# Both scans' output rows turned by VectorE, ahead of the next carry instead of behind it or through TensorE

## The chip, the cores and the metric

The kernel runs on one core of one Trainium2 chip. The time is the device time of one execution in microseconds; the time before is the median of 3 runs. The profile is of one further execution. Engines are named as in the profile: PE (TensorE matmul; PEld its weight loads), DVE (VectorE), ACT (ScalarE), POOL (GpSimd) and SP (SyncE, which here only issues DMAs). A q behind a name (SPq, ACTq) is that engine's issuing side.

## The reference

The input x is 16 images of 64 rows, 128 columns and 64 channels in float32. Two residual blocks follow each other:

```
x = x + mix(groupnorm(x)) + bias     # mix: along the 128 columns, one softmax matrix for each of 4 heads
x = x + scan(groupnorm(x))           # scan over the 64 rows of an image, one after the other

carry = row[0]                       # an output row too
carry = row[h] + relu(conv1d_9(carry))      # h = 1..63: 9 taps along the 128 columns, 64 x 64 channels
```

Both group norms are over the whole image in 32 groups of 2 channels, so a scan can begin only when its images are mixed. Each scan row needs the one before it.

## The kernel before, in words

The images go in two waves of 8. First the 8 images of wave 0 are loaded, normalised and mixed with no scan beside them (until about 183 us). Then wave 0 is scanned, 64 rows for 8 images at once, while the 8 images of wave 1 are loaded, normalised and mixed beside it: one image for each iteration of 8 rows ("the first scan" below). Last, wave 1 is scanned with nothing beside it ("the second scan", from about 548 us). Each engine's program is written out by hand in its own order; engines meet only at semaphores (wait_ge, then_inc). An engine's instructions run in that order, so one that waits holds up all behind it.

Data of a scan row lie with two neighbouring columns times 64 channels on the 128 partitions. A row is split in two halves, s = 0 and s = 1, of 4 images each (NS = 2, SW = 256 elements a partition). For each half of each row:

- PE convolves (convolve, L1037 and L1041): 15 products of 256 columns, five each of wh with carry_h, wl with carry_h, and wh with carry_l. carry_h is the carry written as fp32r, carry_l the rest.
- DVE makes the new carry in L825: the larger of the convolution and 0, plus the normalised row. It waits for conv_done, every fourth row for rows_ready, and for total_ready, which says that the carry before has been read.
- ACT rounds the carry into carry_h (L543); DVE subtracts the two into carry_l (L835).
- POOL adds the carry to the unnormalised row: total (add_carry, L410), the output row. It may overwrite total only when the row before has been turned.
- ACT normalises one image's next group of four rows into rows (norm_rows, L513).

total has columns and channels on the partitions and must be turned before it is stored. Before the change this is done in two ways. In the first scan PE turns row t-1 by four 128 x 128 transposes into ps_out, behind the convolution of half 0 of row t (turn_out, L1029); ACT copies ps_out to staged (stage_out, L523), and SP stores it with two DMAs of 128 KB in pieces of 512 bytes (store_row, L303). In the second scan DVE turns each half in blocks of 32 x 32 (flip_out, L812), right behind the carry of the next row's same half, and the row is stored by eight DMAs of 32 KB in pieces of 128 bytes, five issued by SP (L314) and three by ACT (L533). staged has two buffers, taken in turn, so a turn of row h waits until the stores of row h-2 have landed.

In the first scan DVE has the preparation of the next image between these (prep, with a gap number for its place in the row: gap 0 and 2 behind the carry of half 0 and 1, gap 1 and 3 behind carry_l): statistics (L638, L739), the mixed sum of a quarter image (L732, behind half 1 of odd rows) and small operations for the group norms. PE has the mix (L949) and the turning of the mixed rows (L962) behind half 1, POOL the scaling for the mix (L379), and ACT the copying of the mixed rows (L491).

The order in DVE's program before, around the carry:

```
dve.wait_ge(conv_done[s], t + 1)
...
nc.vector.scalar_tensor_tensor(carry[s][:, :], ...).then_inc(carry_ready[s], 1)
if wave == 1 and not (is_zero(it) and i == 0):
    flip_out(wave, it, i, s)
if b is not None:
    prep(b, e, it, i, 2 * s, prev, more)
if not (last and i == STEPS - 1):
    dve.wait_ge(high_ready[s], t + 2)
    nc.vector.tensor_tensor(carry_l[s]...).then_inc(low_ready[s], 1)
```

Of the kernel before, what the change touches and what calls it, by code (L numbers as in the profile page):

```python
# [15 lines left out]
def mix_and_scan_kernel(nc: bass.Bass, x: bass.AP, centers: bass.AP, spreads: bass.AP,  # L16
# [8 lines left out]
    B, H, N, C = x.shape  # L25
# [33 lines left out]
    out_pairs = out.rearrange("b h (j q) c -> b h j (q c)", q=2)  # L59

    with ExitStack() as ctx:
# [139 lines left out]
        out_turned = sem("out_turned")  # L201
        out_staged = sem("out_staged")
        stored = [sem(f"stored{n}") for n in range(2)]
# [60 lines left out]
        def _(sp):  # L264
# [30 lines left out]
            def store_row(wave, h, t, buf):  # L295

                staged_rows = held(sp, t)
                alone(sp, w_zeroed)
                sp.wait_ge(out_staged, staged_rows)
                src = staged[:, buf, :].rearrange("p (m f) -> p m f", f=P)  # L300
                for e in range(2):
                    dst = out_pairs[wave * W + e:(wave + 1) * W:2, bass.ds(h, 1), :, :]
                    sp.dma_start(dst.rearrange("m h j f -> (h j) m f"),  # L303
                                 src[e * J:(e + 1) * J, :, :]).then_inc(stored[buf], 16)

            def store_flipped(wave, h, buf):

                rows_flipped = held(sp, h + 1)
# [3 lines left out]
                for block in range(SP_BLOCKS):  # L312
                    dst, src = flipped_block(wave, h, buf, block)
                    sp.dma_start(dst, src).then_inc(flip_stored[buf], 16)  # L314

            def iteration(wave, it, b, e, more):


                for i in range(STEPS):
                    if wave == 1 and not (is_zero(it) and i == 0):  # L320
                        store_flipped(wave, it * STEPS + i - 1, (i + 1) % 2)
                    if wave == 0 and not (is_zero(it) and i == 0):
                        store_row(wave, it * STEPS + i - 1, (it + wave * ITERS) * STEPS + i, (i + 1) % 2)
                    if i == 1 and more >= 1:
                        load_chunk(b + 1, 1 - e, CH - 1, CH * b)
                    if i in (3, 5, 7) and more >= 2:
                        load_chunk(b + 2, e, (i - 3) // 2, CH * b + (i - 3) // 2 + 1)

# [7 lines left out]
            store_row(0, H - 1, H, 1)  # L336
# [4 lines left out]
            for n in range(2):  # L341
                sp.wait_ge(stored[n], H // 2 * 32)
                sp.wait_ge(flip_stored[n], H // 2 * 128)
# [3 lines left out]
        def _(pool):  # L347
# [53 lines left out]
            def add_carry(wave, it, i, s):  # L401
                t = (it + wave * ITERS) * STEPS + i
                pool.wait_ge(carry_ready[s], t + 1)
                if wave == 0 and not is_zero(t):
                    pool.wait_ge(out_turned, t)
                if wave == 1 and is_zero(it) and i == 0:
                    pool.wait_ge(out_turned, t)
# [717 lines left out]
```

## Time and profile before

| | |
|---|---|
| median of 3 runs | 787.57 us (785.27 to 787.59) |
| the profiled execution | 787.0 us |
| its span, first to last instruction | 785.2 us |
| mean granted clock of TensorE | 0.978 of full |
| PE, DVE, ACT, POOL busy | 703.5, 580.8, 524.2, 421.0 us |
| transferred | 68.11 MB, 87 GB/s over the span |

The page's list of costliest groups gives for each line and engine the operation, the tiles it writes and reads, the number, the busy time, the mean of one, the idle time ahead of it and what ended that. Lists in order of time give start, length, engine, line, operation and tiles, with the idle time ahead of the first and what ended it in square brackets. The length of an operation runs from its start to its end; an engine may start the next a little before the end of the last, so the distance of two starts is what an operation costs the engine.

### The profile page before, as it was taken

How to read it: one execution, taken by the hardware profiler on the slowest of the kernel's cores; microseconds unless marked ns; L12 is line 12 of the kernel's file. 1: busy time of each engine (PE TensorE's matmuls, PEld its weight loads, DVE VectorE, ACT ScalarE, POOL GpSimd, SP SyncE). 2: the span in 40 equal slices, each digit the busy share in tenths (PEclk: the TensorE clock that was granted, in tenths of full speed). 3: DMA queues.
4: the chain of work that ended last, by engine and by line, in shares of the span. 5: the costliest groups of instructions: out<-in, count | busy, mean ns of one | idle time of the engine just before them, and what ended most of it. 6: DMA issues, size and time to landing. Idle time of an engine off the chain costs nothing.

```text
span 785.2 us, 18039 instructions
## 1 busy us (share of the span) xinstructions
PE 703.5 (90%) x5356; PEld 671.4 (86%) x5356; DVE 580.8 (74%) x1298; ACT 524.2 (67%) x918; POOL 421.0 (54%) x416
## 2 busy tenths in 40 slices
PE   1577777767999999999999999995999999999996
PEld 1466666667999999999999999995999999999996
DVE  7589999955868787786868777664766767777775
ACT  1167767785877777777777777756566666666661
POOL 1555566623655556565656565661455555555553
PEclk9889999998999999999999999998999999999999
DMA  9846556132434443444434431221344444444444
GB/s 179 157 109 133 122 121 134 28 81 49 100 76 101 108 95 84 94 108 94 93 81 107 96 80 43 53 56 27 52 74 76 71 73 74 71 75 68 78 69 80
DMA packets 307594, 68.11 MB, mean 87 GB/s; under 512 B 274772, under 2 KB 307540, under 8 KB 307540
## 3 DMA queue, kind: packets, MB, share of 16 engines
q1 hardware_dynamic: 255316, 61.15, 38.0%
q10 hardware_dynamic: 52224, 6.30, 5.2%
q8 instruction: 26, 0.43, 0.2%
q14 instruction: 28, 0.23, 0.1%
HBM read 33.85 MB, written 33.55 MB: 86 GB/s over the span
## 4 chain that ended last, share of the span: by engine, by line
PE 58%; DVE 15%; issue 11%; ACT 7%; ACTq 6%; POOL 1%; SPq 0%; DVEq 0%; DMA 0%; POOLq 0%
PE ps_conv L1037 26%; PE ps_conv L1041 13%; PE ps_mix L949 9%; PE ps_in L962 6%; ACTq L533 5%; DVE st L638 5%; PE ps_out L1029 3%; ACT x_paired L491 2%; DVE carry L825 2%; ACT carry_h L543 2%; PE ps_small L939 2%; DVE x_sb L732 2%; DVE st L739 2%; ACT rows L513 1%; DVE rows L732 1%
## 5 line engine op out<-in xcount | busy, mean ns | idle before, releaser
L410 POOL TENSOR_TENSOR total<-x_paired,carry 128x256 f32<-128x256 f32 x256 | 234.2, 915 | 256.6 <-DVE carry L825 145.8
L835 DVE TENSOR_TENSOR carry_l<-carry,carry_h 128x256 fp32r<-128x256 f32 x252 | 166.1, 659 | 82.6 <-ACT carry_h L543 74.1
L543 ACT ACTIVATE carry_h<-carry 128x256 fp32r<-128x256 f32 x252 | 105.5, 419 | 162.9 <-DVE carry L825 115.8
L513 ACT ACTIVATE rows<-x_paired,shift,rstd 128x256 f32 (+1 forms) x256 | 213.4, 842 | 0.2
L1037 PE MATMUL ps_conv<-carry_h,wh 128*128 128x256 f32 x1280 | 208.1, 293 | 4.7 <-ACT carry_h L543 4.2
L491 ACT ACTIVATE x_paired<-ps_in,shift 64x512 f32<-64x512 f32 (+1 forms) x256 | 174.8, 683 | 30.2 <-PE ps_in L962 26.0
L1041 PE MATMUL ps_conv<-carry_l,wh 128*128 128x256 f32 x1280 | 194.6, 282 | 0.0
L1037 PE MATMUL ps_conv<-carry_h,wl 128*128 128x256 f32 x1280 | 193.9, 282 | 0.0
L1037 PEld LDWEIGHTS ps_conv<-carry_h,wh 128*128 128x128 f32 x1280 | 170.6, 191 | 8.1 <-ACT carry_h L543 6.9
L379 POOL TENSOR_TENSOR xs<-x_sb,minus_rstd 128x512 f32<-128x512 f32 x104 | 147.9, 1435 | 43.8 <-DVE minus_rstd L714 40.9
L1037 PEld LDWEIGHTS ps_conv<-carry_h,wl 128*128 128x128 f32 x1280 | 171.0, 189 | 0.0
L1041 PEld LDWEIGHTS ps_conv<-carry_l,wh 128*128 128x128 f32 x1280 | 171.0, 189 | 0.0
L825 DVE SCALAR_TENSOR_TENSOR carry<-ps_conv,rows 128x256 f32<-128x256 f32 x256 | 106.6, 417 | 72.9 <-PE ps_conv L1041 62.7
L949 PE MATMUL ps_mix<-xs,mix 128*128 128x256 f32 x384 | 102.2, 397 | 0.0
L739 DVE BATCH_NORM_STATS2 st<-x_paired 128x6 f32<-128x512 f32 (+1 forms) x128 | 85.4, 681 | 8.9 <-ACT x_paired L491 8.9
L949 PEld LDWEIGHTS ps_mix<-xs,mix 128*128 128x128 f32 x384 | 70.6, 199 | 7.2
L638 DVE BATCH_NORM_STATS2 st<-x_sb 128x6 f32<-128x256 f32 x208 | 75.0, 412 | 0.0
L962 PE MATMUL ps_in<-ident,x_sb 128*128 128x128 f32 x416 | 55.4, 277 | 15.5 <-ACT x_paired L491 11.3
L962 PEld LDWEIGHTS ps_in<-ident,x_sb 128*128 128x128 f32 x416 | 48.0, 143 | 22.7 <-issue 19.0
L812 DVE STREAM_TRANSPOSE staged<-total 128x256 f32<-128x256 f32 x128 | 55.4, 433 | 3.6 <-DMA out_dram<-staged 3.4
L732 DVE SCALAR_TENSOR_TENSOR x_sb<-ps_mix,bias_col,x_sb 128x1024 f32<-128x1024 f32 x42 | 53.5, 1274 | 3.2 <-PE ps_mix L949 3.2
L379 POOL TENSOR_TENSOR xs<-rows,minus_rstd 128x512 f32<-128x512 f32 x24 | 31.3, 1334 | 32.7 <-DVE minus_rstd L714 31.2
(92 smaller groups left out, 396.7 us busy)
## 6 DMA issues: line engine op xcount, KB each, us to landing
x_sb<-in_x_dram SPq DMA_DIRECT2D x52, 512.0 KB, 4.2
out_dram<-staged SPq DMA_DIRECT2D x128, 128.0 KB, 2.4
out_dram<-staged SPq DMA_DIRECT2D x320, 32.0 KB, 1.6
rows<-in_x_dram SPq DMA_DIRECT2D x12, 512.0 KB, 4.1
out_dram<-staged ACTq DMA_DIRECT2D x192, 32.0 KB, 1.7
x_paired<-in_L_conv_W_dram SPq DMA_DIRECT2D x2, 80.0 KB, 2.7
x_paired<-in_L_conv_W_dram SPq DMA_DIRECT2D x2, 64.0 KB, 2.5
x_paired<-v_attention_centers_dram SPq DMA_DIRECT2D x1, 0.0 KB
```

Source lines behind the costliest of these rows:

```text
L379: nc.gpsimd.tensor_tensor(xs[:, c % 2, heads, :, :].rearrange("p s h v -> p h v s"), src, minus_rstd1[:, k, m:G:2].unsqueeze(1).unsqueeze( ...
L410: nc.gpsimd.tensor_tensor(total[s][:, :].rearrange("p (w j) -> p w j", w=WS), x1_rows(wave, it, i, 1, s * WS, WS)[:, 0, :, :], carry[s][:, ...
L491: ins = nc.scalar.activation(dst[q * C:(q + 1) * C, r:CR:2, :], src[:, q, :, :], ACT.Identity, bias=shift1[r * C:(r + 1) * C, k:k + 1])
L513: nc.scalar.activation(rows[:, g % 2, :, w // WS, :, w % WS], x1_rows(wave, it, g * RG, RG, w, 1)[:, :, 0, :], ACT.Identity, scale=rstd2[: ...
L543: nc.scalar.activation(carry_h[s][:, EDGE:EDGE + J, :].rearrange("p j w -> p (j w)"), carry[s][:, :], ACT.Copy).then_inc(high_ready[s], 1)
L638: ins = nc.vector.bn_stats(st1[:, 0, 2 * m:2 * m + 2, :].rearrange("p g k -> p (g k)"), v[:, m, :, :, :])
L825: nc.vector.scalar_tensor_tensor(carry[s][:, :], ps_conv[:, s * BANK:s * BANK + SW], 0.0, rows[:, (i // RG) % 2, i % RG, s, :, :].rearrang ...
L835: nc.vector.tensor_tensor(carry_l[s][:, EDGE:EDGE + J, :].rearrange("p j w -> p (j w)"), carry[s][:, :], carry_h[s][:, EDGE:EDGE + J, :].r ...
L949: ins = nc.tensor.matmul(ps[:, s * CR * V:(s + 1) * CR * V], mix[:, s, :], xs[:, c % 2, s, :, :].rearrange("p h v -> p (h v)"), start=True ...
L962: ins = nc.tensor.transpose(ps_in[:, k * P:(k + 1) * P], x_bufs[e][:, at:at + P], ident[:, :])
L1037: nc.tensor.matmul(ps_conv[:, s * BANK:s * BANK + SW], w[:, d, :], carry_h[s][:, d:d + J, :].rearrange("p j w -> p (j w)"), start=(w is wh ...
L1041: ins = nc.tensor.matmul(ps_conv[:, s * BANK:s * BANK + SW], wh[:, d, :], carry_l[s][:, d:d + J, :].rearrange("p j w -> p (j w)"), start=F ...
```

## The change

In both scans the row is now turned by DVE in 32 x 32 blocks. In DVE's program the turn of row t-1 stands ahead of the wait for the convolution of row t, so ahead of the carry of row t, no longer behind it. PE's transposes of output rows, ACT's copy of them and the store in 512-byte pieces are gone. In the first scan SP issues all eight stores of a row, in the second SP five and ACT three as before. SP's loads of the coming images now stand ahead of the row's stores. The semaphores out_turned, out_staged and stored are gone; out_flipped and flip_stored count through both scans. The last row of the first scan is turned behind the clearing of the carries, ahead of the last image's statistics. Some of the small operations of an image's preparation move: PE's var1_of of the seventh row from half 0 to half 1, ACT's std1_of likewise, ACT's square1_of to the eighth row, DVE's guess1_of to the eighth row behind the first carry, and ratio1_of and rstd1_of behind the second carry of that row, together with mean_rstd1.

```diff
...
@@ -292,24 +288,13 @@
             for c in range(CH - 1):
                 load_chunk(W + 1, 1, c, CH * (W - 1) + c + 1)
-            def store_row(wave, h, t, buf):
-
...
             def store_flipped(wave, h, buf):
-                rows_flipped = held(sp, h + 1)
+                rows_flipped = held(sp, wave * H + h + 1)
                 alone(sp, w_zeroed)
                 for s in range(NS):
                     sp.wait_ge(out_flipped[s], rows_flipped)
-                for block in range(SP_BLOCKS):
+                for block in range(BLOCKS if wave == 0 else SP_BLOCKS):
                     dst, src = flipped_block(wave, h, buf, block)
                     sp.dma_start(dst, src).then_inc(flip_stored[buf], 16)
@@ -317,14 +302,12 @@
                 for i in range(STEPS):
-                    if wave == 1 and not (is_zero(it) and i == 0):
-                        store_flipped(wave, it * STEPS + i - 1, (i + 1) % 2)
-                    if wave == 0 and not (is_zero(it) and i == 0):
-                        store_row(wave, it * STEPS + i - 1, (it + wave * ITERS) * STEPS + i, (i + 1) % 2)
                     if i == 1 and more >= 1:
                         load_chunk(b + 1, 1 - e, CH - 1, CH * b)
                     if i in (3, 5, 7) and more >= 2:
                         load_chunk(b + 2, e, (i - 3) // 2, CH * b + (i - 3) // 2 + 1)
+                    if not (is_zero(it) and i == 0):
+                        store_flipped(wave, it * STEPS + i - 1, (i + 1) % 2)
...
@@ -401,12 +383,8 @@
             def add_carry(wave, it, i, s):
                 t = (it + wave * ITERS) * STEPS + i
                 pool.wait_ge(carry_ready[s], t + 1)
-                if wave == 0 and not is_zero(t):
-                    pool.wait_ge(out_turned, t)
-                if wave == 1 and is_zero(it) and i == 0:
-                    pool.wait_ge(out_turned, t)
-                if wave == 1 and not (is_zero(it) and i == 0):
-                    pool.wait_ge(out_flipped[s], it * STEPS + i)
+                if not is_zero(t):
+                    pool.wait_ge(out_flipped[s], t)
...
-            def stage_out(t, buf):
-
-                act.wait_ge(out_turned, t)
-                if not (isinstance(t, int) and t <= 2):
-
-                    act.wait_ge(stored[buf], (t - 1 - buf) * 16)
-                nc.scalar.activation(staged[:, buf, :], ps_out[:, :], ACT.Copy).then_inc(out_staged, 1)
-
...
@@ -543,25 +513,23 @@
                             nc.scalar.activation(carry_h[s][:, EDGE:EDGE + J, :].rearrange("p j w -> p (j w)"),
                                                  carry[s][:, :],
                                                  ACT.Copy).then_inc(high_ready[s], 1)
-                        if s == 0 and wave == 0 and not begins:
-                            stage_out(t, (i + 1) % 2)
                         g = i // RG + 1
                         if not (last and g == GROUPS):
                             norm_rows(wave, it + g // GROUPS, g % GROUPS, (i % RG) * NS + s)
-                        if s == 0 and i == 6 and more:
+                        if s == 1 and i == 6 and more:
                             std1_of(b + 1)
+                        if s == 0 and i == 7 and more:
+                            square1_of(b + 1)
...
                     if i == 5 and more:
                         dev2_of(b + 1)
-                    if i == 6 and more:
-                        square1_of(b + 1)
...
@@ -784,12 +751,11 @@
                         stats1(b + 1, 1 - e, 6 + 3 * gap // 2, 3)
                     if i == 5 and gap < 2:
                         stats1(b + 1, 1 - e, 12 + 2 * gap, 2)
-                    if i == 6 and gap == 2:
+                    if i == 7 and gap == 0:
                         guess1_of(b + 1)
-                    if i == 7 and gap == 0:
+                    if i == 7 and gap == 2:
                         ratio1_of(b + 1)
                         rstd1_of(b + 1, 1 - e)
-                    if i == 7 and gap == 2:
                         mean_rstd1(b + 1, 1 - e)
                 if i == 0 and gap == 0 and prev:
                     keep_shift1(b, e)
@@ -805,10 +771,8 @@
                 buf = (i + 1) % 2
                 h = it * STEPS + i - 1
-                if isinstance(h, int) and h < 2:
-                    dve.wait_ge(stored[buf], H // 2 * 32)
-                else:
-                    dve.wait_ge(flip_stored[buf], 128 * (it * (STEPS // 2) + (i - 1) // 2))
+                if not (wave == 0 and isinstance(h, int) and h < 2):
+                    dve.wait_ge(flip_stored[buf], 128 * (wave * H // 2 + it * (STEPS // 2) + (i - 1) // 2))
                 nc.vector.transpose(staged[:, buf, s * SW:(s + 1) * SW],
                                     total[s][:, :]).then_inc(out_flipped[s], 1)
@@ -817,17 +781,17 @@
                 for i in range(STEPS):
                     t = (it + wave * ITERS) * STEPS + i
                     for s in range(NS):
+                        if not is_zero(t):
+                            dve.wait_ge(total_ready[s], t)
+                        if not (is_zero(it) and i == 0):
+                            flip_out(wave, it, i, s)
                         dve.wait_ge(conv_done[s], t + 1)
                         if i % RG == 0:
                             dve.wait_ge(rows_ready, W // RG * t + W)
-                        if not is_zero(t):
-                            dve.wait_ge(total_ready[s], t)
                         nc.vector.scalar_tensor_tensor(
                             carry[s][:, :], ps_conv[:, s * BANK:s * BANK + SW], 0.0,
                             rows[:, (i // RG) % 2, i % RG, s, :, :].rearrange("p j w -> p (j w)"),
                             ALU.max, ALU.add).then_inc(carry_ready[s], 1)
-                        if wave == 1 and not (is_zero(it) and i == 0):
-                            flip_out(wave, it, i, s)
                         if b is not None:
                             prep(b, e, it, i, 2 * s, prev, more)
                         if not (last and i == STEPS - 1):
@@ -912,6 +876,9 @@
                 nc.vector.memset(carry_h[s][:, :, :].bitcast(f32), 0.0).then_inc(high_ready[s], 1)
                 nc.vector.memset(carry_l[s][:, :, :].bitcast(f32), 0.0).then_inc(low_ready[s], 1)
+            for s in range(NS):
+                dve.wait_ge(total_ready[s], H)
+                flip_out(0, ITERS, 0, s)
...
@@ -988,13 +955,12 @@
             def prep(b, e, i, after, prev, more):
-                if after == 0:
-                    if i == 6 and more:
-                        var1_of(b + 1, inv_p[:, :], 1)
-                else:
+                if after == 1:
                     mix_half(b, i // 2, i % 2, ps_mix, b * CH + i // 2)
                     if i == 0 and prev:
                         turn_in(b - 1, 1 - e, CH - 1)
+                    if i == 6 and more:
+                        var1_of(b + 1, inv_p[:, :], 1)
...
@@ -1019,17 +985,6 @@
                 mean2_of(b, wave)
                 var2_of(b, wave)
-            def turn_out(t):
-
-                if not (isinstance(t, int) and t <= 1):
-                    pe.wait_ge(out_staged, t - 1)
-                for s in range(NS):
-                    pe.wait_ge(total_ready[s], t)
-                    for m in range(WS // 2):
-                        ins = nc.tensor.transpose(ps_out[:, s * SW + m * P:s * SW + (m + 1) * P],
-                                                  total[s][:, m * P:(m + 1) * P], ident[:, :])
-                ins.then_inc(out_turned, 1)
-
...
@@ -1048,8 +1003,6 @@
                     for s in range(NS):
                         if not (i == 0 and is_zero(it)):
                             convolve(t, s)
-                            if s == 0 and wave == 0:
-                                turn_out(t)
                         if b is not None:
                             prep(b, e, i, s, prev, more)
...
```

## Rows read from the trace of the kernel before

**Rows 1.** The page, busy time, share of the span and instructions of each engine.
```profile
PE 703.5 (90%) x5356; PEld 671.4 (86%) x5356; DVE 580.8 (74%) x1298; ACT 524.2 (67%) x918; POOL 421.0 (54%) x416
```
**Rows 2.** Stretches: us, busy (instructions) of PE, PEld, DVE, ACT, POOL, PEclk, DMA share, GB/s.
```profile
227.60:272.00 44.40, 44.28 (x352) 42.79 (x352) 33.05 (x70) 34.34 (x62) 26.26 (x25) 1.00 0.43 96
552.13:775.86 223.73, 223.29 (x1862) 221.38 (x1862) 160.86 (x372) 140.31 (x242) 118.38 (x124) 1.00 0.45 72
```
**Rows 3.** DVE's waits in the first scan: us in total, times, longest us.
```profile
DVE carry L825 <- PE ps_conv L1041: 50.5, 62, 1.9
DVE carry_l L835 <- ACT carry_h L543: 37.8, 89, 0.5
```
**Rows 4.** PE in order of time, first scan: start us, us, line, operation.
```profile
297.52 0.60 PE L1029 MATMUL ps_out<-ident,total 128*128 128x128 f32 x4
297.88 0.84 PE L1037 MATMUL ps_conv<-carry_h,wh 128*128 128x256 f32 x5
```
**Rows 5.** DVE in order of time, second scan, around a turn.
```profile
571.73 0.45 DVE L812 STREAM_TRANSPOSE staged<-total 128x256 f32<-128x256 f32 x1 [1.07 <-DMA out_dram<-staged]
572.10 0.38 DVE L835 TENSOR_TENSOR carry_l<-carry,carry_h 128x256 fp32r<-128x256 f32 x1
```
**Rows 6.** DVE in order of time, first scan, two small operations.
```profile
309.81 0.19 DVE L707 SCALAR_TENSOR_TENSOR ps_small<-ps_small,square 128x32 f32<-128x32 f32 x1
310.03 0.19 DVE L714 SCALAR_TENSOR_TENSOR minus_rstd<-ps_small,guess 128x32 f32<-128x32 f32 x1
```
**Rows 7.** All engines in order of time, second scan, a half row.
```profile
702.70 0.41 DVE L825 SCALAR_TENSOR_TENSOR carry<-ps_conv,rows 128x256 f32<-128x256 f32 x1
...
703.04 0.43 DVE L812 STREAM_TRANSPOSE staged<-total 128x256 f32<-128x256 f32 x1
703.15 0.42 ACT L543 ACTIVATE carry_h<-carry 128x256 fp32r<-128x256 f32 x1 [0.29 <-DVE carry L825]
...
703.60 0.42 DVE L835 TENSOR_TENSOR carry_l<-carry,carry_h 128x256 fp32r<-128x256 f32 x1
703.70 1.05 POOL L410 TENSOR_TENSOR total<-x_paired,carry 128x256 f32<-128x256 f32 x1 [1.21 <-DVE staged L812]
703.71 1.39 ACTq L533 DMA_DIRECT2D out_dram<-staged  x3
```
**Rows 8.** SP's stores: issue ns min/median/max, landing us; two issues of L314, two of L303.
```profile
L314 SPq DMA_DIRECT2D out_dram<-staged x320: 315/316/2336, 555.2 to 783.1; - x160
...
DMA to landing us min/median/max: 1.5/1.6/3.8
...
700.68 0.82 SPq L314 DMA_DIRECT2D out_dram<-staged  x2
...
299.31 1.39 SPq L303 DMA_DIRECT2D out_dram<-staged  x2
```
**Rows 9.** All engines in order of time, the first row of the second scan.
```profile
547.60 0.42 DVE L825 SCALAR_TENSOR_TENSOR carry<-ps_conv,rows 128x256 f32<-128x256 f32 x1 [1.92 <-ACT rows L513]
...
549.37 0.41 DVE L825 SCALAR_TENSOR_TENSOR carry<-ps_conv,rows 128x256 f32<-128x256 f32 x1
...
549.96 0.89 POOL L410 TENSOR_TENSOR total<-x_paired,carry 128x256 f32<-128x256 f32 x1 [0.80 <-DVE carry L825]
...
550.26 0.88 DVE L835 TENSOR_TENSOR carry_l<-carry,carry_h 128x256 fp32r<-128x256 f32 x1 [0.48 <-ACT carry_h L543]
```
**Rows 10.** POOL and then DVE in order of time, first scan, around one carry_l.
```profile
323.20 0.87 POOL L410 TENSOR_TENSOR total<-x_paired,carry 128x256 f32<-128x256 f32 x1 [1.30 <-DVE carry L825]
...
323.51 0.84 DVE L835 TENSOR_TENSOR carry_l<-carry,carry_h 128x256 fp32r<-128x256 f32 x1 [0.48 <-ACT carry_h L543]
324.28 1.27 DVE L732 SCALAR_TENSOR_TENSOR x_sb<-ps_mix,bias_col,x_sb 128x1024 f32<-128x1024 f32 x1
```
**Rows 11.** ACT in order of time, between the scans.
```profile
539.37 0.60 ACT L523 ACTIVATE staged<-ps_out 128x512 f32<-128x512 f32 x1
...
539.99 4.41 ACT L513 ACTIVATE rows<-x_paired,shift,rstd 128x256 f32<-128x256 f32 x7
```

More of the change, by code:

```diff
@@ L58, in mix_and_scan_kernel @@
     out_blocks = out.rearrange("b h (jh jl q) c -> b h jh jl q c", jl=BL, q=2)
-    out_pairs = out.rearrange("b h (j q) c -> b h j (q c)", q=2)
     with ExitStack() as ctx:
@@ L200, in mix_and_scan_kernel @@
         total_ready = [sem(f"total_ready{s}") for s in range(NS)]
-        out_turned = sem("out_turned")
-        out_staged = sem("out_staged")
-        stored = [sem(f"stored{n}") for n in range(2)]
         out_flipped = [sem(f"out_flipped{s}") for s in range(NS)]
@@ L293, in _ @@
                 load_chunk(W + 1, 1, c, CH * (W - 1) + c + 1)
-            def store_row(wave, h, t, buf):
[L297 to L304, printed above, removed]
             def store_flipped(wave, h, buf):
-                rows_flipped = held(sp, h + 1)
+                rows_flipped = held(sp, wave * H + h + 1)
                 alone(sp, w_zeroed)
@@ L335, in _ @@
                 iteration(0, ITERS - 2 + e, B - 2 + e, e, 1 - e)
-            store_row(0, H - 1, H, 1)
+            store_flipped(0, H - 1, 1)
             iteration(1, 0, None, None, 0)
@@ L341, in _ @@
             for n in range(2):
-                sp.wait_ge(stored[n], H // 2 * 32)
-                sp.wait_ge(flip_stored[n], H // 2 * 128)
+                sp.wait_ge(flip_stored[n], H * 128)
         @block.gpsimd
@@ L515, in norm_rows @@
                                      bias=shift2[:, b:b + 1]).then_inc(rows_ready, 1)
-            def stage_out(t, buf):
-                act.wait_ge(out_turned, t)
-                if not (isinstance(t, int) and t <= 2):
-                    act.wait_ge(stored[buf], (t - 1 - buf) * 16)
-                nc.scalar.activation(staged[:, buf, :], ps_out[:, :], ACT.Copy).then_inc(out_staged, 1)
             def store_flipped(wave, h, buf):
-                rows_flipped = held(act, h + 1)
+                rows_flipped = held(act, wave * H + h + 1)
                 alone(act, setup_done)
@@ L557, in iteration @@
                     if wave == 1 and not begins:
-                        store_flipped(1, it * STEPS + i - 1, (i + 1) % 2)
+                        store_flipped(wave, it * STEPS + i - 1, (i + 1) % 2)
                     if b is not None:
@@ L604, in _ @@
             keep_in(B - 1, 1, 1, W - 1, CH - 1, 0, 4, H)
-            stage_out(H, 1)
             for w in range(W - 1):
@@ L1094, in _ @@
                 iteration(0, ITERS - 2 + e, B - 2 + e, e, True, e == 0)
-            turn_out(H)
             finish(B - 1, 1, 1)
```

## The prediction

> **What bounds the kernel now.** I read the page's engine shares first, then the table of stretches, then DVE's waits and the instruction lists of one or two rows in each scan. PE is busy for 90% of the span [rows 1], so it looks as if only PE's work counted. The stretches say where: in one iteration of the first scan PE works 44.28 of 44.40 us (8 rows, 5.55 us a row), and in the second scan 223.29 of 223.73 us [rows 2]. The second scan's stretch runs from the carry of row 1 to that of row 63, 62 rows, so 3.609 us a row. DVE is busy for 33.05 of 44.40 us and 160.86 of 223.73 us in the same stretches [rows 2], which seems to leave it room for more. But busy is not all that an engine working in order spends: in the first scan DVE stands for only 50.5 us on PE's convolution, and 37.8 us on ACT's carry_h inside a row's own chain [rows 3]. Only the first kind is room for work that stands ahead of the carry. The question of this change is therefore how long DVE's chain of one half row becomes, against 1.80 us of PE per half in the second scan (3.609 / 2) and 2.78 in the first (5.55 / 2).
>
> **First scan, what goes from PE.** Four transposes of a row (L1029) begin at 297.52 and the next convolution at 297.88 [rows 4]: 0.36 us a row of PE, 63 rows and a last one: 22.7 us if PE stayed the bound. ACT's copy of 0.58 us a row goes too; ACT waits for DVE's carry there, so this is worth nothing by itself.
>
> **First scan, what comes to DVE.** Two turns a row. A turn lasts 0.43 us, but operations overlap: where nothing is waited for, the next begins 0.37 us after the turn began (571.73 to 572.10) [rows 5]. 126 turns x 0.37 = 46.6 us. Standing ahead of the wait for the convolution they can use up the 50.5 us in which DVE waits for it [rows 3], and the 0.36 us a row that PE gives back shorten those waits in the same measure as the convolution comes earlier. So DVE replaces PE as what bounds the scan: 46.6 - 50.5 = -3.9 us if no wait for PE is left. Two things push back. At the end of each image's preparation three small operations (ratio, rstd, mean x rstd) now stand together after the second carry of the eighth row, so PE gets its mean x rstd later, behind the mix of that row, and starts the next convolution later; two operations more, at 0.22 us each (309.81 to 310.03) [rows 6], are 0.4, of which PE's slack should take a little: an estimate of 0.3 us for each of 7 images, 2 us. And the DVE turn now waits for stores two rows back: 2 us, next paragraph. I take 0 for the first scan. Bounds: turns at the 0.34 us by which a turn follows a carry (702.70 to 703.04) [rows 7] give 126 x 0.34 - 50.5 = -7.7; turns at their full 0.43 us give +3.7, and with a fifth of the PE waits (10 us) surviving, +13.
>
> **First scan, stores.** SP issued two stores of a row; now it issues eight of 32 KB. One takes 0.316 us to issue and 1.6 to land, and two take 0.82 [rows 8], so they begin 0.50 us apart. Eight take 4.0 us, with a load every second row (0.4 us, ahead of the stores now, so it no longer waits behind them) about 4.2 of the 5.5 us of a row: SP keeps up. The last store lands some 0.5 + 4.0 + 1.6 = 6.1 us after the second half's turn; that buffer is turned into again a row and a half later, 8.2 us. So the turn waits only where SP stops for about 2 us or more, which it can: the longest issue is 2.3 us [rows 8]. A few such stops at the first pass of each loop, 2 us in all. The transfer engines are busy 0.43 of the time in the first scan (2.4 us a row) and 0.45 in the second (1.6 us a row, all of it stores in 128-byte pieces) [rows 2]; both together are at most 4.0 of 5.5 us. The Trainium skill (DMA: Bandwidth & Descriptors, Specifications) gives 512 bytes as the least piece for full rate, and says that smaller ones are read, modified and written; 512-byte pieces are what the first scan gives up. The trace has the 128-byte pieces at the second scan's price just given, so this rule adds to one rival below and not to the sum.
>
> **Second scan, the turn moved ahead.** Now a half goes: carry (L825), turn (L812), carry_l (L835). At 702.70 the carry begins; the turn fills 703.04 to 703.47, while ACT makes carry_h (703.15 to 703.57); carry_l begins at 703.60 and takes 0.42 us; POOL's total begins only at 703.70, because it may not overwrite a row that is not yet turned [rows 7]. So the turn costs DVE nothing: it fills the wait for carry_h, and it holds POOL back until carry_l has started. Behind it, both go. POOL's total starts as soon as the carry is there, 0.59 us after the carry began (549.37 to 549.96), before ACT has carry_h; and carry_l then takes 0.88 us, to 551.14, 0.29 us after POOL's end at 550.85 [rows 9]. That is row 0 of the second scan, before which nothing is turned: the order after the change, less the turn. The first scan shows the same: total 323.20 to 324.07, carry_l until 324.35, 0.28 us later, next DVE operation 0.07 us before that, at 324.28 [rows 10]. So a half costs DVE, per turn and carry: 0.37 (turn) + 0.59 (carry to POOL's start) + 0.87 (total) + 0.28 - 0.07 = 2.04, with the extra waits of the turn I take 2.05 us. That is over PE's 1.80. DVE becomes the bound at 4.10 us a row: 62 x (4.10 - 3.609) = 30.4 us lost. Bounds: 2.00 us (4.00 a row, no overlap lost anywhere) gives 24; the 1.77 us between the two carries of that same row 0 (547.60 to 549.37) [rows 9] and 0.37 give 2.14, so 4.28 a row and 42.
> ACT's stores in this scan are no new bound: their three issues take 1.39 us [rows 7] and could delay carry_h by a tenth or so, but carry_l waits for POOL some 0.4 us past carry_h anyway.
> The Trainium skill has the rule for this in SBUF — State Buffer, "Who interferes with whom": a VectorE instruction with two SBUF inputs and a GpSimd instruction that reads SBUF exclude each other, and the one issued first keeps the other out until it ends. It speaks against this change, which lets POOL go first. Taken strictly, carry_l would run its whole 0.42 us after POOL's end, a half would be 2.19 us, and the scan would lose 48 us; the rows show 0.28.
>
> **Between the scans.** ACT copies the last row (0.60 us, 539.37) right before the seven normalised rows that the second scan's first carry waits for [rows 11]; that copy goes: -0.6 us. DVE's two turns stand there beside ACT's work and cost nothing.
>
> **Sum.** The profiled execution took 787.0 us (span 785.2), the median of the runs is 787.57, 0.6 more, so no correction is needed. 787.0 + 0 + 30.4 - 0.6 = 816.8; I say 817.
>
> **Rivals.**
> A, PE stays the bound in both scans: the turns fill waits for the convolution and carry_l doesn't wait for POOL. Then the second scan goes to PE's pure pace, six groups of five products begun 0.59 us apart (3.54 us a row, 62 x -0.07 = -4.3), and the first gains the 22.7: 787.0 - 4.3 - 22.7 - 0.6 = 759. For it: PE's 90%, and 50.5 us of waiting for PE. Against it [rows 9, 10]: each carry_l behind POOL's total.
> B, stores hold the turns back in the first scan, slower still: if SP's small stores there cost the 0.69 us of its large ones (two in 1.39 us) [rows 8], or transfers mixed with loads go slower, eight need 5.5 us, with loads 5.8 a row instead of 5.5; the turn, and the carry queued behind it, waits for a buffer in every row: 63 x 0.27 = 17 more, 834. It decides once SP's eight issues and the load exceed a row. For it: loads and stores share SP's queue; against it the 0.50 us at which they followed in the second scan [rows 8].
> C, the first scan gains all of PE's 22.7 since the turns fall into DVE's waits just where these are, while the second loses as forecast: 794. For it: in several rows DVE waits over 1 us before the carry; against it: other halves have no wait, and there a turn is pushed in whole.
> D, the two scans cancel: the first gains C's amount, the second loses 22 (just under its lower bound): no change.
>
> **Chances.** Forecast 0.66 (its own range 802 to 829, from -8 and 24 below and, above, +13 with the loss as taken), B 0.12, C 0.11, A 0.09, D 0.02. What this kernel's runs can tell from no change is about 0.3%, 2.4 us. Slower 0.66 + 0.12 + 0.11 = 0.89, same 0.02, faster 0.09. The range runs from 797, which leaves out A, D and half of C, to 836, which takes in B's price and most of its spread and the 42 of the second scan's bound short of the first's +13: some 0.18 is left out.
>
> **What would show it.** In the second scan carries 4.1 us apart per row, carry_l at about 0.8 us with its end 0.28 us after POOL's, hardly any wait of DVE for PE, and PE busy for some 86% (3.54 / 4.10) where it was 99.8%. In the first scan iterations of 44 to 45 us, with DVE's wait for PE near zero and no transposes into ps_out. It is wrong if carry_l stays at 0.42 us in the second scan (then A), if turns wait for stores in the first scan row after row (B), if its iterations fall to 42 us (C), or if PE's granted clock drops below 1.00 in the second scan because it now pauses in each half row.

## The result, and the profile after

798.42 us against 786.42 before: 1.0149 times the time (95% interval 1.0119 to 1.0178), 12 us slower. (One of the four executions after took 1339.87 us; it stands in the median and not in the ratio, and without it the median is 797.76.) The forecast was slower by 30, so the sign and the place of the loss were right and the size was not. The profiled execution after took 797.43 us, its span is 795.6.

Where the time went is read from DVE's list: the carries mark the stages. "Opening" is the start of the first carry; each scan is counted from its row to its last row as named; "end" is from the last row's first carry to the end of the span.

| us | opening | first scan, 64 rows | between | second scan, rows 1 to 63 | a row of it | end | span |
|---|---|---|---|---|---|---|---|
| before | 183.2 | 349.9 | 14.45 | 223.7 | 3.61 | 9.3 | 785.2 |
| after | 180.5 | 340.1 | 13.85 | 249.1 | 4.02 | 7.6 | 795.6 |
| difference | -2.75 | -9.84 | -0.60 | +25.35 | | -1.74 | +10.4 |

(Row 0 to row 1 of the second scan takes 4.5 us in both.) The opening runs the same program in both kernels; its 2.75 us are not the change's, see the last section.

Next come lines to set beside those of before: the page's first line (to [rows 1]) and stretches (to [rows 2]): the whole first scan, one iteration of it, and the second scan. Each stretch gives us, busy by engine in the order PE, PEld, DVE, ACT, POOL, then PEclk, DMA share, GB/s. After:

```profile
PE 699.4 (88%) x5100; PEld 647.3 (81%) x5100; DVE 639.5 (80%) x1426; ACT 490.8 (62%) x854; POOL 408.9 (51%) x416
...
180.46:520.56 340.10, 324.43 (x2485) 308.72 (x2486) 292.56 (x652) 231.80 (x405) 205.11 (x196) 0.99 0.47 86
265.12:309.01 43.89, 41.56 (x320) 39.28 (x320) 38.59 (x87) 30.32 (x53) 26.23 (x25) 1.00 0.52 95
538.95:788.03 249.08, 247.30 (x1869) 228.99 (x1869) 186.63 (x372) 140.31 (x242) 107.37 (x124) 1.00 0.41 65
```

Before, the whole first scan:

```profile
183.21:533.15 349.94, 347.61 (x2737) 336.34 (x2738) 260.07 (x526) 264.73 (x468) 206.00 (x196) 0.99 0.38 85
```

PE now pauses in the first scan (324.43 of 340.10 us). In the second it still shows as busy, though a row that holds 3.54 us of products takes 4.02: the profile models the ends of matmuls, and five products that showed 0.75 us in the second scan before can now show 0.85 (at 700.89 us, below). PE's granted clock is 1.00 there, as before. Waits of DVE (to [rows 3]) and of PE in the first scan after:

```profile
DVE carry_l L799 <- ACT carry_h L513: 41.0, 84, 0.7
DVE carry L791 <- PE ps_conv L996: 4.8, 13, 1.0
...
DVE staged L776 <- DMA out_dram<-staged: 0.2, 1, 0.2
...
PE ps_small L906 <- DVE minus_mean_rstd L686: 7.6, 7, 1.3
PE ps_small L906 <- DVE st L605: 6.0, 7, 0.9
```

DVE's wait for the convolution has gone from 50.5 to 4.8 us, and PE waits for what DVE prepares for the next image: DVE bounds the first scan. The wait for stores is 0.2 us in all.

The second scan after, all engines in order of time (to [rows 7] and [rows 9]):

```profile
699.64 0.43 DVE L776 STREAM_TRANSPOSE staged<-total 128x256 f32<-128x256 f32 x1
...
700.01 0.38 DVE L791 SCALAR_TENSOR_TENSOR carry<-ps_conv,rows 128x256 f32<-128x256 f32 x1
...
700.42 0.42 ACT L513 ACTIVATE carry_h<-carry 128x256 fp32r<-128x256 f32 x1 [0.85 <-DVE carry L791]
700.58 0.86 POOL L388 TENSOR_TENSOR total<-x_paired,carry 128x256 f32<-128x256 f32 x1 [1.14 <-DVE carry L791]
...
700.87 0.85 DVE L799 TENSOR_TENSOR carry_l<-carry,carry_h 128x256 fp32r<-128x256 f32 x1 [0.48 <-ACT carry_h L513]
...
700.89 0.85 PE L992 MATMUL ps_conv<-carry_h,wh 128*128 128x256 f32 x5
...
701.65 0.43 DVE L776 STREAM_TRANSPOSE staged<-total 128x256 f32<-128x256 f32 x1
702.01 0.38 DVE L791 SCALAR_TENSOR_TENSOR carry<-ps_conv,rows 128x256 f32<-128x256 f32 x1
```

This is the chain of the forecast, link by link. The turn puts the carry 0.37 us later. POOL's total starts 0.57 us after the carry began, lasts 0.86 and ends at 701.44; carry_l, shown from 700.87 on, ends at 701.72, 0.28 us later. The next carry begins 2.00 us after this one, and PE's 1.77 us a half no longer decide.

### The profile page after: what moved, and what is told of

It is laid out like the page before. It is cut to its first block, busy times and chain, and to the rows that moved or that the text cites. A ratio compares the mean times of both kernels' runs of the same rounds, so it can differ in the third digit from the quotient of the medians.

```text
span 795.6 us, 18259 instructions
## 1 busy us (share of the span) xinstructions
PE 699.4 (88%) x5100; PEld 647.3 (81%) x5100; DVE 639.5 (80%) x1426; ACT 490.8 (62%) x854; POOL 408.9 (51%) x416
## 4 chain that ended last, share of the span: by engine, by line
DVE 32%; PE 29%; issue 19%; ACT 8%; SPq 6%; ACTq 2%; DMA 1%; DVEq 1%; POOL 1%; POOLq 0%
PE ps_conv L992 15%; DVE st L605 8%; PE ps_conv L996 7%; DVE staged L776 6%; SPq L299 6%; DVE carry L791 5%; ACT carry_h L513 4%; DVE st L706 4%; PE ps_mix L916 3%; DVE x_sb L699 3%; PE ps_in L929 3%; ACTq L503 2%; ACT rows L491 2%; ACT x_paired L469 2%; DVE carry_l L799 1%
## 5 line engine op out<-in xcount | busy, mean ns | idle before, releaser
L388 POOL TENSOR_TENSOR total<-x_paired,carry 128x256 f32<-128x256 f32 x256 | 222.0, 867 | 283.0 <-DVE carry L791 282.4
L799 DVE TENSOR_TENSOR carry_l<-carry,carry_h 128x256 fp32r<-128x256 f32 x252 | 195.9, 777 | 103.9 <-ACT carry_h L513 103.9
L992 PE MATMUL ps_conv<-carry_h,wh 128*128 128x256 f32 x1280 | 214.6, 298 | 7.2 <-ACT carry_h L513 6.5
L776 DVE STREAM_TRANSPOSE staged<-total 128x256 f32<-128x256 f32 x256 | 109.5, 428 | 0.8 <-DMA out_dram<-staged 0.7
L791 DVE SCALAR_TENSOR_TENSOR carry<-ps_conv,rows 128x256 f32<-128x256 f32 x256 | 98.1, 383 | 10.3 <-PE ps_conv L996 6.3
L916 PE MATMUL ps_mix<-xs,mix 128*128 128x256 f32 x384 | 99.3, 389 | 0.5
L916 PEld LDWEIGHTS ps_mix<-xs,mix 128*128 128x128 f32 x384 | 68.3, 193 | 7.9 <-POOL xs L361 1.4
```

Of the source, the lines that this page charges most:

```text
L388: nc.gpsimd.tensor_tensor(total[s][:, :].rearrange("p (w j) -> p w j", w=WS), x1_rows(wave, it, i, 1, s * WS, WS)[:, 0, :, :], carry[s][:, ...
L776: nc.vector.transpose(staged[:, buf, s * SW:(s + 1) * SW], total[s][:, :]).then_inc(out_flipped[s], 1)
L791: nc.vector.scalar_tensor_tensor(carry[s][:, :], ps_conv[:, s * BANK:s * BANK + SW], 0.0, rows[:, (i // RG) % 2, i % RG, s, :, :].rearrang ...
L799: nc.vector.tensor_tensor(carry_l[s][:, EDGE:EDGE + J, :].rearrange("p j w -> p (j w)"), carry[s][:, :], carry_h[s][:, EDGE:EDGE + J, :].r ...
L916: ins = nc.tensor.matmul(ps[:, s * CR * V:(s + 1) * CR * V], mix[:, s, :], xs[:, c % 2, s, :, :].rearrange("p h v -> p (h v)"), start=True ...
L992: nc.tensor.matmul(ps_conv[:, s * BANK:s * BANK + SW], w[:, d, :], carry_h[s][:, d:d + J, :].rearrange("p j w -> p (j w)"), start=(w is wh ...
```

## Experiments

The stages of each are from its own trace; the median is over its executions, and the ratio is to executions of the kernel before that were taken with it.

| us | opening | first scan | second scan | a row of it | end | median | ratio to before (interval) |
|---|---|---|---|---|---|---|---|
| e1: second scan behind | 183.3 | 339.8 | 227.2 | 3.67 | 9.4 | 779.09 | 0.990 (0.985 to 0.994) |
| e2: POOL waits, second | 180.6 | 340.1 | 222.5 | 3.59 | 7.9 | 775.06 | 0.985 (0.981 to 0.990) |
| e3: POOL waits, both | 183.4 | 328.4 | 221.3 | 3.57 | 7.9 | 761.55 | 0.968 (0.964 to 0.973) |
| e4: behind in both | 184.8 | 337.9 | 226.6 | 3.65 | 9.4 | 777.62 | 0.987 (0.982 to 0.992) |
| e5: e3, turns behind | 180.7 | 332.3 | 220.9 | 3.56 | 9.3 | 763.65 | 0.971 (0.969 to 0.974) |
| e7: turn twice | 180.9 | 383.4 | 288.7 | 4.66 | 7.9 | 882.51 | 1.122 (1.118 to 1.127) |
| e8: small turn, first | 181.2 | 326.8 | 249.1 | 4.02 | 7.6 | 785.66 | 0.999 (0.997 to 1.001) |
| e9: small turn, second | 183.6 | 339.9 | 222.2 | 3.58 | 7.8 | 773.04 | 0.982 (0.979 to 0.984) |
| e10: before, second ahead | 180.5 | 351.5 | 252.4 | 4.07 | 7.6 | 812.71 | 1.033 (1.031 to 1.035) |

**e1, the turn behind the carry in the second scan only.**

```diff
-                        if not (is_zero(it) and i == 0):
+                        if not (is_zero(it) and i == 0) and not (wave == 1):
                             flip_out(wave, it, i, s)
                         dve.wait_ge(conv_done[s], t + 1)
...
                             ALU.max, ALU.add).then_inc(carry_ready[s], 1)
+                        if not (is_zero(it) and i == 0) and (wave == 1):
+                            flip_out(wave, it, i, s)
```

> The changed kernel with one part undone: in the second scan the turn stands behind the carry again, in the first scan it stays ahead. Theory (the turn's place decides the second scan: behind the carry it fills DVE's wait for carry_h and holds POOL's total back until carry_l has started): the second scan goes back from 4.02 to 3.61 us a row, 62 rows, 25 us less, so about 772 us, 14 below the kernel before, since the first scan keeps its 340 us. Rival (what is lost is not the turn's place but the stores, ACT's issues or SP): the second scan stays near 4.0 us a row and the time near 797.

The second scan is back at 3.67 us a row, 22 us less than the changed kernel's; the first is unchanged (339.8). The place of the turn decides the second scan; the rival falls. The total, 779.09, is 7 above the 772 expected: the row takes 0.06 us more than in the kernel before, the end is again 9.4 us, and the opening was a long one.

**e2, the turn stays ahead, POOL waits for carry_l in the second scan.**

```diff
                 if not is_zero(t):
                     pool.wait_ge(out_flipped[s], t)
+                if (wave == 1) and not (is_last(it) and i == STEPS - 1):
+                    pool.wait_ge(low_ready[s], t + 2)
...
-            with pool.Fori(0, ITERS) as it:
+            with pool.Fori(0, ITERS - 1) as it:
                 iteration(1, it, None, None, False, False)
+            iteration(1, ITERS - 1, None, None, False, False)
```

The last row has no carry_l to wait for, so POOL's last iteration stands behind its loop; e3 and e5 have this too.

> The changed kernel with the turn ahead in both scans as it is, but in the second scan POOL's total waits until carry_l is written. Theory (the price is carry_l standing behind POOL's total): a half costs DVE 0.36 (turn) + 0.86 (carry to carry_l's start) + 0.43 - 0.07 = 1.58 us, below PE's 1.77, so PE is the bound again at 3.54 us a row: 30 us less than the changed kernel, about 768. Rival (the price is the turn itself in a longer chain, and carry_l takes 0.84 us in any case): a half stays at 2.0 us, the time near 797, or above where POOL's later total makes the turn wait.

3.59 us a row (3.54 expected) with the turn still ahead, and 775.06 us in all (768 expected). DVE and POOL in order of time:

```profile
700.60 0.42 DVE L802 TENSOR_TENSOR carry_l<-carry,carry_h 128x256 fp32r<-128x256 f32 x1 [0.48 <-ACT carry_h L516]
700.94 0.44 DVE L779 STREAM_TRANSPOSE staged<-total 128x256 f32<-128x256 f32 x1
701.29 0.86 POOL L390 TENSOR_TENSOR total<-x_paired,carry 128x256 f32<-128x256 f32 x1 [0.77 <-DVE carry_l L802]
701.30 0.38 DVE L794 SCALAR_TENSOR_TENSOR carry<-ps_conv,rows 128x256 f32<-128x256 f32 x1
```

carry_l takes 0.42 us instead of 0.85, and the next carry begins 0.70 us after carry_l did, not 1.14. So the turn ahead is not dear by itself: with it there, what POOL does decides. Whether POOL's total ahead of carry_l is dear by itself is the question of the next run.

**e9, a small turn in the second scan,** separates the two parts of that chain.

```diff
+            nc.vector.memset(staged[:, :, :], 0.0)
...
-                nc.vector.transpose(staged[:, buf, s * SW:(s + 1) * SW],
-                                    total[s][:, :]).then_inc(out_flipped[s], 1)
+                n = SW if wave == 0 else 32
+                nc.vector.transpose(staged[:, buf, s * SW:s * SW + n],
+                                    total[s][:, 0:n]).then_inc(out_flipped[s], 1)
```

> The changed kernel, but in the second scan a turn handles 32 of its 256 elements a partition (the rest of the row is left out, so 0 or older rows are stored there); stores and waits stay. Theory (the second scan is lost by two things together, the turn on DVE's chain and carry_l behind POOL's total, which only add up to more than PE's pace): a half falls from 2.00 to about 1.64 + 0.12 = 1.76 us, just at PE's 1.77, so about 3.6 us a row, 225 us in place of 249, about 773 in all. Rival (carry_l behind POOL's total is enough by itself, the turn counts for little): 3.9 us a row or more, 790 or more.

DVE in order of time:

```profile
701.60 0.20 DVE L778 STREAM_TRANSPOSE staged<-total 128x32 f32<-128x32 f32 x1
701.73 0.38 DVE L793 SCALAR_TENSOR_TENSOR carry<-ps_conv,rows 128x256 f32<-128x256 f32 x1
702.59 0.84 DVE L801 TENSOR_TENSOR carry_l<-carry,carry_h 128x256 fp32r<-128x256 f32 x1 [0.48 <-ACT carry_h L513]
703.36 0.20 DVE L778 STREAM_TRANSPOSE staged<-total 128x32 f32<-128x32 f32 x1
703.49 0.38 DVE L793 SCALAR_TENSOR_TENSOR carry<-ps_conv,rows 128x256 f32<-128x256 f32 x1
```

carry_l takes 0.84 us behind POOL's total, as in the changed kernel, yet the half is 1.76 us and the row 3.58. So neither part alone costs anything here; the turn and the wait for POOL are lost only because together they pass PE's pace.

**e10, that one part of the change put into the kernel before** (the turn ahead of the wait for the convolution in the second scan; the first scan with PE's transposes and ACT's copy).

```diff
+                        if not is_zero(t):
+                            dve.wait_ge(total_ready[s], t)
+                        if wave == 1 and not (is_zero(it) and i == 0):
+                            flip_out(wave, it, i, s)
                         dve.wait_ge(conv_done[s], t + 1)
...
-                        if not is_zero(t):
-                            dve.wait_ge(total_ready[s], t)
...
-                        if wave == 1 and not (is_zero(it) and i == 0):
-                            flip_out(wave, it, i, s)
```

> The kernel before with one part of the change alone: in the second scan the turn stands ahead of the carry; the first scan keeps PE's turning and ACT's copy. Theory (the two scans' changes are independent): the first scan stays at 350 us, the second goes from 3.61 to 4.02 us a row, 25 us more, less 1.8 at its end: 787.3 + 23.5 = 811. Rival (the loss in the second scan comes with something else of the change, such as the order of loads and stores or what stands in the loops): about 787.

812.71 us: the move alone costs 25 us over the 787.23 of the kernel before, and the rest of the change brings some 14 back (812.71 to 798.42). In the trace the second scan grows by 28.7 us, 4.07 us a row where 4.02 was expected.

**e8, a small turn in the first scan** (as e9, with `wave == 1` in the condition).

> The changed kernel, but in the first scan a turn handles 32 of its 256 elements a partition (the rest of the row is left out, so 0 is stored there); the stores and all waits stay. Theory (the turns made DVE the bound of the first scan and ate half of what PE gained): a turn falls to about 0.1 us, 16 halves gain some 4 us an iteration until PE bounds it at 41.6 us: 328 instead of 340 us, the second scan unchanged, 786 in all. Rival (stores of 128-byte pieces or SP's eight issues hold the first scan): it stays at 340, 797 in all.

The first scan falls to 326.8 us, 23.1 below the kernel before: about what PE's transposes were worth (22.7 forecast; PE shows 26.1 us less of busy time and 3.0 more of idle time). The stores and SP's eight issues are still there, so they don't hold it. The turns at full size cost 340.1 - 326.8 = 13.3 of these 23.

**e7, every turn twice,** the first time into a bank of PSUM that nobody reads during the scans.

```diff
+                nc.vector.transpose(ps_out[:, s * SW:(s + 1) * SW], total[s][:, :])
                 nc.vector.transpose(staged[:, buf, s * SW:(s + 1) * SW],
```

> The changed kernel with every turn made twice, the first time into a bank of PSUM that nobody reads. Theory (DVE bounds both scans and a turn costs its whole 0.36 us): 126 turns more make the first scan about 45 us longer (385), 124 more the second about 45 (294): about 888 us in all. Rival (the first scan still has room for turns in waits for PE): the first scan grows by 30 us or less; and if the second scan were held by something beside DVE's chain, it would grow by less than 40.

The first scan grows by 43.3 us for 126 turns (0.34 each), the second by 39.6 for 124 (0.32). In time order, a half row of the second scan:

```profile
699.95 0.45 DVE L776 STREAM_TRANSPOSE ps_out<-total 128x256 f32<-128x256 f32 x1
700.31 0.40 DVE L777 STREAM_TRANSPOSE staged<-total 128x256 f32<-128x256 f32 x1
700.63 0.38 DVE L792 SCALAR_TENSOR_TENSOR carry<-ps_conv,rows 128x256 f32<-128x256 f32 x1
```

A second turn adds 0.32 us: the one that follows it takes 0.40 instead of 0.45. The first scan has no room left on DVE, as the theory has it. The second's 39.6 falls just under the 40 that was set for its rival; the 0.32 us from the second turn's start to the carry's, 124 times, account for it without one. Later in e7's first scan PE's granted clock falls to 0.50, the low one of its two levels (1.2 GHz), in five stretches of 3.4 us (the first at 223.8), which no other run shows there; PE had worked only 1.7 to 1.9 of the 4 us before each. DVE waits 6.0 us for PE in that scan, so little of the 43.3 can be PE's.

**e3, POOL waits for carry_l in both scans** (as e2, with `wave in (0, 1)`).

> As the run with POOL waiting for carry_l in the second scan, and in the first scan too. Theory: the first scan, where DVE is the bound at about 43.9 us an iteration, loses up to 0.42 us in the halves that have nothing else between carry and carry_l, and becomes bound by PE at about 41.6 us an iteration: some 2 us for each of 8 iterations, 330 instead of 340 us; 757 to 760 in all. Rival (DVE in the first scan is bound by its own operations, not by the wait for POOL, or POOL's scaling comes too late for PE's mix when its total is put off): no gain in the first scan or a loss, 768 or more.

The first scan loses another 11.7 us (340.1 to 328.4), and the whole runs in 761.55 us, 3.2% below the kernel before: the best version found. Its waits in the first scan:

```profile
POOL total L390 <- DVE carry_l L802: 135.3, 121, 2.8
...
DVE carry L794 <- PE ps_conv L999: 19.4, 29, 1.8
...
DVE staged L779 <- DMA out_dram<-staged: 5.1, 7, 1.4
```

DVE waits for PE again, and now, at shorter rows, for stores too (5.1 us).

**e4, the turn behind the carry in both scans** (e1's move for both waves).

> The changed kernel with the turn behind the carry in both scans, all else as changed. Theory (the place of the turn decides): the turn fills the wait for carry_h where nothing else stands there and holds POOL back, so in the first scan DVE's chain shortens by up to 0.7 us in such halves and PE becomes the bound, about 41.6 us an iteration, 330 us; the second scan goes to 3.61 us a row; some 760 in all. Rival (in the first scan the turn ahead was hidden in the wait for the convolution and costs nothing, so putting it behind the carry makes the chain longer): the first scan takes 340 us or more, 772 or more in all.

The second scan is as expected (3.65), the first is not: 337.9, where the theory had 330 and the rival 340 or more; neither gives this number. Two carry_l of its first scan, in a row without and a row with statistics ahead of carry_l:

```profile
275.97 0.43 DVE L801 TENSOR_TENSOR carry_l<-carry,carry_h 128x256 fp32r<-128x256 f32 x1
...
285.08 0.43 DVE L776 STREAM_TRANSPOSE staged<-total 128x256 f32<-128x256 f32 x1
285.44 0.71 DVE L605 BATCH_NORM_STATS2 st<-x_sb 128x6 f32<-128x256 f32 x2
286.07 0.84 DVE L801 TENSOR_TENSOR carry_l<-carry,carry_h 128x256 fp32r<-128x256 f32 x1
```

Where statistics stand between, the turn only delays POOL until it meets carry_l after all. DVE stands 47.5 us waiting for PE in this scan, so it is not simply DVE's sum. PE waits too:

```profile
PE ps_small L908 <- DVE st L605: 7.3, 7, 1.1
PE ps_small L908 <- DVE minus_mean_rstd L686: 5.2, 7, 0.8
```

These are PE's small products for the next image's group norm. PE waits 12.5 us for what DVE owes them, and 3.0 us in e3 (0.5 and 2.5); the first scans of the two runs lie 9.5 us apart. So in some rows DVE waits for PE and in others PE for DVE. That this is the whole of the missing 8 us is a reading of the traces; no run tests it.

**e5, e3 with the turns behind the carry.**

> As the run with POOL waiting for carry_l in both scans (761.6 us), but the turn stands behind the carry in both. Theory (with POOL held back explicitly the turn's place matters only by the wait for carry_h that it can fill): DVE's half is shorter by 0.36 us where nothing else stands between carry and carry_l, but the second scan is bound by PE already (3.57 us a row) and the first nearly so, so 0 to 5 us less, 757 to 762. Rival (the turn ahead is better because it fills the wait for the convolution, and behind the carry it delays carry_l and by that PE): 3 us or more above 761.6.

763.65 us; its interval overlaps e3's, so the totals don't tell them apart. In the traces its first scan is 4 us longer (332.3), which leans to the rival: with POOL held back, the turn ahead uses waits for the convolution that the turn behind does not (DVE waits 49.3 us for it here and 19.4 in e3).

## Why the prediction was wrong in size

- **PE bound before, DVE after:** right in both scans (waits above, e7).
- **PE's 22.7 us in the first scan:** right, 23.1 (e8).
- **"I take 0 for the first scan":** this is the step that failed. The scan gained 9.84 us. The mechanism was right, DVE replacing PE as the bound; the term for what the turns add to DVE was too large, 46.6 us. In the stretches above, DVE's busy time grew by only 32.5 us (260.07 to 292.56), while its idle time fell by 42.3 (89.87 to 47.54: waits for the convolution 45.7 less, for carry_h 3.2 more); the two make the 9.84. The turns themselves were nearly right: 0.36 us from start to start, 45.4 for 126. DVE's groups in the first scan (x number | busy us, mean ns | idle us before them and what ended it), before and then after:

```profile
L835 DVE TENSOR_TENSOR carry_l<-carry,carry_h 128x256 fp32r<-128x256 f32 x126 | 94.4, 749 | 37.9 <-ACT carry_h L543 37.8
L825 DVE SCALAR_TENSOR_TENSOR carry<-ps_conv,rows 128x256 f32<-128x256 f32 x128 | 53.1, 415 | 52.7 <-PE ps_conv L1041 50.5 <-ACT rows L513 1.9
```

```profile
L799 DVE TENSOR_TENSOR carry_l<-carry,carry_h 128x256 fp32r<-128x256 f32 x126 | 90.0, 714 | 41.0 <-ACT carry_h L513 41.0
L776 DVE STREAM_TRANSPOSE staged<-total 128x256 f32<-128x256 f32 x126 | 53.5, 425 | 0.2 <-DMA out_dram<-staged 0.2
L791 DVE SCALAR_TENSOR_TENSOR carry<-ps_conv,rows 128x256 f32<-128x256 f32 x128 | 49.3, 385 | 6.9 <-PE ps_conv L996 4.8 <-ACT rows L491 1.9
```

Three things were left out of the sum. An operation that follows another without a wait is shorter: after the change a carry that waited took 0.425 us and one that did not 0.38, and the carries went from 0.415 to 0.385 us in the mean, 3.8 us for 128. carry_l, whose length holds its wait for POOL, went from 0.749 to 0.714, 4.4 us. And a start that waits loses the 0.07 us of overlap with the operation before; 49 waits fewer (62 to 13) are 3.4, an estimate. With 0.8 us of others they explain 12.4 of the 12.9 between 45.4 and 32.5.
- **2 us for stores in it:** 0.2. That SP keeps up was right. By the Trainium skill (DMA: Bandwidth & Descriptors, Specifications) pieces below 512 bytes don't reach the full rate. The trace agrees so far: with about the same GB/s (85 and 86) the share of the transfer engines rose from 0.38 to 0.47 in this scan. No time hung on it.
- **2 us for the later mean x rstd:** where PE bounds the scan, in e8, PE waits 3.0 us for it in seven waits, which is about the size taken.
- **30.4 us in the second scan:** the chain was right and 25.35 was measured. A half is 2.00 us, not 2.05: carry 0.38 instead of 0.41, so POOL starts at 0.57 instead of 0.59, and the turn costs 0.36. It is the lower bound that was named.
- **carry_l behind POOL:** shown by e2 (0.42 us there, 0.85 here). The strict reading of the Trainium skill's rule (SBUF — State Buffer, "Who interferes with whom") would have it run its whole 0.42 us after POOL's end; here too it ended 0.28 after. That the one issued first holds the other up agrees, and it holds the other way round as well: in [rows 7], where carry_l came first, POOL's total took 1.05 us, and 0.86 here.
- **"So the turn costs DVE nothing", before:** this was read from half 1 of a row. In half 1 carry_l took 0.43 us in the mean of 62; in half 0 it waited for carry_h in 58 of 62 and took 0.70, since ACT stood at the issue of its stores first (carry_h waited for the turn 49 times, 45.8 us in all). PE's pace hid that; the forecast does not hang on it.
- **Between the scans:** right, -0.60.
- **The end:** not seen. The last row has no carry_l, so its second carry follows 1.0 us after the first, where PE's pace gave 1.8, and less stands behind it, since a turn is done already: the end is 1.74 us shorter. It goes with the turn's place: 7.6 to 7.9 us in every run with the turn ahead, 9.3 to 9.4 with it behind.
- **Rivals:** A fell with carry_l at 0.85, B with the 0.2 us of waiting for stores. C was nearer than thought: the first scan kept 10 of its 23 us.
- **The sum:** of the 19.4 us between 816.8 and the 797.43 measured, the first scan has 9.8, the second 5.1, the end 1.7, and the opening 2.75, which belongs to no kernel. 798.42 us lies below the forecast's own 802 to 829. That it lies inside the wider 797 to 836 is luck: the lower end was set to take in half of rival C.

## What to carry to other kernels

A turn or a copy may cost its engine nothing because it fills a wait and because it holds another engine back. Before moving it, ask what it releases, and whether that meets the next instruction in line. And where one engine replaces another as the bound and the two sums differ by a few per cent, take the new engine's sum from distances from start to start of operations that do not wait. Lengths and idle times read from a trace in which that engine still waits make its new chain look too long.

## What the runs showed of the hardware

The opening takes 180.5 to 181.2 us in some executions and 183.2 to 184.8 in others, with the same program. TensorE's mean granted clock from 20 to 60 us goes with it. Before, and after:

```profile
20.00:60.00 40.00, 26.85 (x118) 22.62 (x118) 27.76 (x62) 15.06 (x27) 21.02 (x16) 0.87 0.69 135
```

```profile
20.00:60.00 40.00, 25.72 (x133) 22.07 (x134) 30.05 (x68) 16.94 (x31) 20.97 (x16) 0.96 0.72 138
```

Before, PE is idle from 32 to 36 us, and from 36 to 40 us the granted clock is 0.50 (1.2 GHz, the low one of its two levels); it is low once more around 50 us (0.61 from 48 to 52). After, PE works 0.13 us from 32 to 36, the mean from 36 to 40 is 0.64, and it is 1.00 from 40 to 60. e1, e3, e4 and e9 show 0.87 or 0.88 and 183.3 to 184.8; e2, e5, e7, e8 and e10 show 0.96 and 180.5 to 181.2. It follows no edit. Executions of the kernel before differ in the same way: those with a mean clock of 0.982 or 0.983 took 784.5 to 785.7 us, those with 0.978 took 787.1 to 788.0. So comparisons of single profiles here carry some 3 us that are no kernel's own.
